# Sparse and linear attention kernel: parts split in PSUM, bf16 bias rows, small PSUM banks re-ordered, one ScalarE instruction for the masked tiles of a unit

## The reference

```python
xn = layernorm(x)
q, k, v = split(xn @ Wqkv.T + bqkv)          # 16 heads of 8
q, k = layernorm(q, q_gamma, q_beta), layernorm(k, k_gamma, k_beta)
aw = softmax(q @ k.T / sqrt(8))
mask = aw >= 12th largest of its row          # top 5% of 256 keys
o_s = (aw * mask / (sum(aw * mask) + 1e-8)) @ v
qf, kf = softmax(q, -1), softmax(k, -1)       # over the 8 channels
o_l = qf @ (kf.T @ v) / (qf . sum(kf) + 1e-6)
o = a * o_s + (1 - a) * o_l                   # a = sigmoid(alpha) per head
y = x + (o @ Wproj.T + bproj) + (xn @ W[idx] + b[idx])
```

## Time and profile before

| | |
|---|---|
| Runs | 1337.95 us median of 3 (1335.01 to 1338.44) |
| Profiled execution, its own time | 1329.16 us |
| Its span, from the first to the last instruction | 1327.4 us |
| Mean granted TensorE clock | 0.926 of full speed |
| Busy share of the span: PE, DVE, ACT, POOL | 79%, 91%, 86%, 82% |
| Bytes moved, mean rate | 83.42 MB, 63 GB/s |

### The profile page before, as it was taken

How to read it: one execution, slowest core, us unless ns; L and a number is a source line. 1 busy time by engine, 2 the same in 40 slices (tenths; PEclk the granted TensorE clock), 3 DMA queues, 4 the chain that set the end, 5 groups by cost and what they waited for, 6 DMA issues and landing times.

```text
span 1327.4 us, 39880 instructions
## 1 busy us (share of the span) xinstructions
PE 1051.5 (79%) x9156; PEld 718.5 (54%) x9156; DVE 1212.3 (91%) x4660; ACT 1135.2 (86%) x3946; POOL 1092.6 (82%) x1618
## 2 busy tenths in 40 slices
PE   3578887878787888887888887788878888887887
PEld 1345555555555555555555555555555555555555
DVE  5789999999899998999989999899989999999994
ACT  3588998998899897998888989788988889998984
POOL 4588888988789887889878889788888888889973
PEclk9979999998899998998989989889998889899998
DMA  2212221222222122221112222112221122221220
GB/s 57 68 45 73 76 77 43 60 65 65 79 77 70 36 64 65 77 77 52 56 53 75 77 77 60 46 53 77 77 79 34 58 65 77 76 77 37 61 58 13
DMA packets 165196, 83.42 MB, mean 63 GB/s; under 512 B 7747, under 2 KB 164933, under 8 KB 164934
## 3 DMA queue, kind: packets, MB, share of 16 engines
q1 hardware_dynamic: 164934, 80.54, 21.1%
HBM read 42.77 MB, written 37.75 MB: 61 GB/s over the span
## 4 chain that ended last, share of the span: by engine, by line
PE 34%; issue 21%; ACT 17%; POOL 13%; DVE 13%; DVEq 1%; POOLq 1%; ACTq 0%; DMA 0%; SPq 0%
PE turn_ps L814 9%; ACT e L705 9%; POOL below L389 8%; DVE rest L510 6%; PE turn_ps L815 4%; DVE top L503 4%; PE work_ps L892 3%; PE work_ps L891 3%; PE pv_ps L831 3%; DVE next L516 3%; PE score_ps L797 2%; PE pv_ps L843 2%; ACT xn L756 2%; PE work_ps L921 2%; ACT below L718 1%
## 5 line engine op out<-in xcount | busy, mean ns | idle before, releaser
L389 POOL TENSOR_SCALAR below<-e,next 128x256 bf16<-128x256 f32 x768 | 695.8, 921 | 0.0
L705 ACT ACTIVATE e<-score_ps,drop 128x256 f32<-128x256 f32 x1024 | 475.4, 492 | 76.1 <-POOL drop L363 75.6
L814 PE MATMUL turn_ps<-ident,e 128*128 128x128 f32 x2048 | 432.8, 304 | 29.1 <-issue 14.5
L510 DVE MATCH_REPLACE8 rest<-e 128x256 f32<-128x256 f32 x1024 | 413.1, 406 | 0.9 <-issue 0.9
L516 DVE MAX8 next<-rest 128x8 f32<-128x256 f32 x1024 | 410.5, 411 | 3.3 <-issue 1.8
L815 PE MATMUL turn_ps<-minus_huge,below 128*128 128x128 bf16 x2048 | 406.4, 234 | 0.0
L503 DVE MAX8 top<-score_ps 128x8 f32<-128x256 f32 x1024 | 360.2, 413 | 37.3 <-PE score_ps L797 19.8
L814 PEld LDWEIGHTS turn_ps<-ident,e 128*128 128x128 f32 x2048 | 314.4, 154 | 97.9 <-issue 31.5
L666 ACT ACTIVATE kept<-turn_ps 128x512 f32<-128x512 f32 x512 | 292.2, 624 | 67.0 <-PE turn_ps L815 62.6
L815 PEld LDWEIGHTS turn_ps<-minus_huge,below 128*128 128x128 bf16 x2048 | 234.7, 115 | 0.0
L705 ACT ACTIVATION_READ_ACCUMULATOR e<-score_ps,drop 128x1 f32 x1024 | 229.3, 224 | 0.0
(11 more groups left out here) (141 smaller groups left out, 1529.7 us busy)
## 6 DMA issues: line engine op xcount, KB each, us to landing
part_slots<-part SPq DMA_DIRECT2D x128, 192.0 KB, 2.3
q_slots<-part_slots SPq DMA_DIRECT2D x64, 256.0 KB, 3.4
k_slots<-part_slots SPq DMA_DIRECT2D x64, 256.0 KB, 4.2
part_slots<-part SPq DMA_DIRECT2D x64, 128.0 KB, 1.9
x_sb<-in_L_attn_x SPq DMA_DIRECT2D x32, 128.0 KB, 4.0
x_res<-in_L_attn_x SPq DMA_DIRECT2D x32, 128.0 KB, 3.9
out_y<-out_sb SPq DMA_DIRECT2D x32, 128.0 KB, 4.3
w_ops<-in_L_ffn_W SPq DMA_DIRECT2D x1, 512.0 KB
```

The lines of the kernel that those rows point to most:

```text
L389: nc.gpsimd.tensor_scalar(below[:, r, t, :], e[:, r, t, :], next8[:, r, t, TOPK - 9:TOPK - 8], None, ALU.is_lt).then_inc(s["below_pool"], 1)
L510: nc.vector.match_replace(rest[:, t, :], e8[:, (u_ - 1) % 2, t, :], e[:, (u_ - 1) % RING, t, :], REMOVED).then_inc(s["rest_ready"], 1)
L705: nc.scalar.activation(e[:, u_ % RING, t, :], score_ps[:, u_ % 2, t // 2, t % 2, :], ACT.Exp, bias=drop[:, u_ % 2, t, 0:1], accum_out=z[:, ...
L814: mm(dst, e[:, r, t, keys], ident[:], start=True, stop=False, is_transpose=True)
```

## The change

- **Parts in PSUM.** `qkT` and `residue` and POOL's two subtractions are gone. ACT casts the first part from `work_ps`; PE then adds minus that part into the same bank (a bf16 matrix with -1 on its diagonal, 512 columns), and ACT casts the second part from there; once more for the third. The transposes into the bank are one accumulation group.
- **Biases.** The three fp32 rows become rows of three partitions holding three bf16 parts of each bias, multiplied by a 3 by 128 block of ones, one bf16 matmul each. DVE makes the parts in the set-up, seven instructions per row (`in_parts`), two of the three rows in `stage_gate`.
- **One sums step.** Both halves of the tokens are transposed in unit 5 (eight transposes, through a permutation that packs nine columns per head, so that both halves fit one bank), and it stands after the scores in PE's list. DVE's three operations are done once, on both halves.
- **Order of the small banks.** The transposed q features go from unit 4 to unit 0, their product from unit 5 to unit 2 (DVE reads it in unit 3, slots 1 and 3, before PE may transpose q and k). The output goes to `pv_ps`: its transposes stay in unit 1, its products go from unit 2 (after the scores) to unit 3 (before the scores).
- **Evacuation.** `kept` of a unit is one instruction over both banks of `turn_ps`, 1024 columns. PE starts a unit's masked tiles when that instruction has ended, and the instruction starts when all of them are there.

```diff
-                        for hh in range(2):
-                            act.wait_ge(s["turn_ready"], 2 * (g - 4) + hh + 1)
-                            nc.scalar.activation(kept[:, u_ % 4, hh], turn_ps[:, hh], ACT.Relu).then_inc(
-                                s["turn_copied"], 1)
+                        act.wait_ge(s["turn_ready"], g - 3)
+                        nc.scalar.activation(kept[:, u_ % 4], turn_ps[:], ACT.Relu).then_inc(s["turn_copied"], 1)
...
-                        wait(act, s["residue_ready"], 2 * (it + 1))
-                        nc.scalar.copy(qkT[:], work_ps[:].rearrange("p (a n) -> p a n", a=2)).then_inc(
-                            s["qkT_copied"], 1)
...
-                    if u_ == 4 and exists(it):
+                    if u_ == 0 and exists(it):
                         act.wait_ge(s["w_qfT"], it + 1)
+                        wait(act, s["w_lin"], it)
                         nc.scalar.copy(qfT[:], work_ps[:, 0:N]).then_inc(s["qfT_copied"], 1)
                     if u_ in (4, 5) and exists(it + 1):
                         p = u_ - 3
-                        act.wait_ge(s["residue_ready"], 2 * (it + 1) + p)
-                        nc.scalar.copy(part[:, p], residue[:, p - 1]).then_inc(s["part_ready"], 1)
+                        act.wait_ge(s["w_rest"], 2 * (it + 1) + p)
+                        nc.scalar.copy(part[:, p], work_ps[:].rearrange("p (a n) -> p a n", a=2)).then_inc(
+                            s["part_ready"], 1)
```

On DVE (set-up and `extra`):

```diff
+            def in_parts(row, cols):
+                p0, p1 = bias_part[:, 0, cols], bias_part[:, 1, cols]
+                r1, r2, total = bias_rest[:, 0, cols], bias_rest[:, 1, cols], bias_sum[:, cols]
+                own = [ident[0:PARTS, p:p + 1] for p in range(PARTS)]
+                setup(nc.vector.tensor_copy(p0, row))
+                setup(nc.vector.tensor_tensor(r1, row, p0, ALU.subtract))
+                setup(nc.vector.tensor_copy(p1, r1))
+                setup(nc.vector.tensor_tensor(r2, r1, p1, ALU.subtract))
+                setup(nc.vector.tensor_scalar(total, p0, own[0], None, ALU.mult))
+                setup(nc.vector.scalar_tensor_tensor(out=total, in0=p1, scalar=own[1], in1=total, op0=ALU.mult,
+                                                     op1=ALU.add))
+                return nc.vector.scalar_tensor_tensor(out=bias3[:, cols], in0=r2, scalar=own[2], in1=total,
+                                                      op0=ALU.mult, op1=ALU.add)
...
-                    if u_ == 5 and 3 <= k <= 5 and exists(it):
+                    if u_ == 3 and k in (1, 3) and exists(it):
...
-                    if u_ in (5, 7) and 1 <= k <= 4 and exists(it - 1):
+                    if u_ == 5 and 1 <= k <= 4 and exists(it - 1):
```

On PE (`mm` is a matmul, `early` comes before the scores of a unit, `late` after):

```diff
                     pe.wait_ge(s["below_act"], (TILES - POOL_TILES) * (g2 + 1))
+                    wait(pe, s["turn_copied"], g2)
                     for hh in range(2):
-                        wait(pe, s["turn_copied"], 2 * (g2 - 1) + hh + 1)
...
+                def sums():
+                    pe.wait_ge(s["pv_copied"], QUADS * it)
+                    for t in range(NT):
+                        for q in range(QUADS):
+                            at = (t * QUADS + q) * 4 * VA
+                            last = nc.tensor.transpose(pv_ps[:, at:at + P], oT[:, nxt, q, t * P:(t + 1) * P], gather[:])
+                    last.then_inc(s["w_turn"], 1)
+                def remainder(p):
+                    pe.wait_ge(s["part_ready"], PARTS * (it + 1) + p + 1)
+                    mm(work_ps[:], minus_one[:], part[:, p].rearrange("p a n -> p (a n)"), start=False,
+                       stop=True, skip_group_check=True).then_inc(s["w_rest"], 1)
...
+                    if u_ == 0 and exists(it):
+                        pe.wait_ge(s["dexp_ready"], 2 * it + 1)
+                        if exists(it + 1):
+                            pe.wait_ge(s["raw_ready"], it + 2)
...
+                    if u_ == 3 and exists(it - 2):
+                        pe.wait_ge(s["osT_copied"], it - 1)
+                        pe.wait_ge(s["pv_copied"], QUADS * it - 1 if exists(it - 1) else QUADS * B)
...
+                            mm(dst, ones3[:], bias3[:, 3 * C:4 * C], start=False, stop=False)
...
+                    if u_ == 5 and exists(it + 1):
+                        remainder(1)
                     if u_ == 6 and exists(it + 1):
...
-                        wait(pe, s["part_ready"], PARTS * (it + 1) + 1)
-                        wait(pe, s["lin_ready"], it + 1)
+                        pe.wait_ge(s["part_ready"], PARTS * (it + 2))
...
-                    if u_ in (5, 7) and exists(it - 1):
-                        sums(u_)
                     early(u_)
                     if exists(it if u_ < UNITS - 1 else it + 1):
                         scores(u_)
+                    if u_ == 5 and exists(it - 1):
+                        sums()
                     late(u_)
```

More of the change, by code:

```diff
@@ L185, in build @@
         oT = sb("oT", [P, 2, QUADS, N])
-        den = sb("den", [P, 2, NT, H])
+        den = sb("den", [P, 2, NT * H])
         o_sparse = sb("o_sparse", [P, NT, C])
@@ L862, in early @@
+                        last.then_inc(s["w_qfT"], 1)
+                    if u_ == 1 and exists(it - 2):
+                        pe.wait_ge(s["osp_ready"], it - 1)
+                        pe.wait_ge(s["lin_ready"], it - 1)
+                        pe.wait_ge(s["pv_copied"], QUADS * it - 2 if exists(it - 1) else QUADS * B)
+                        for t in range(NT):
+                            dst = pv_ps[:, t * P:(t + 1) * P]
                             mm(dst, o_sparse[:, t, :], ident[:], start=True, stop=False, is_transpose=True)
@@ L880, in early @@
                             mm(dst, xnT[:, (xr + 1) % XRING, t * P:(t + 1) * P], w_v[:], start=True, stop=False)
-                            last = mm(dst, ones_row[:], b_row[:, 2 * C:3 * C], start=False, stop=True)
+                            last = mm(dst, ones3[:], bias3[:, 2 * C:3 * C], start=False, stop=True)
                         last.then_inc(s["w_v_ready"], 1)
@@ L891, in early @@
                             mm(dst, xnT[:, (xr + 2) % XRING, t * P:(t + 1) * P], w_qk[:], start=True, stop=False)
-                            last = mm(dst, ones_row[:], b_row[:, 0:2 * C], start=False, stop=True)
+                            last = mm(dst, ones3[:], bias3[:, 0:2 * C], start=False, stop=True)
                         last.then_inc(s["w_qk_ready"], 1)
@@ L929, in late @@
                             for t in range(NT):
-                                last = nc.tensor.transpose(
-                                    work_ps[:, side * N + t * P:side * N + (t + 1) * P],
-                                    qkn[:, (2 * t + side) * C:(2 * t + side + 1) * C], ident[:])
+                                first = side == 0 and t == 0
+                                last = mm(work_ps[:, side * N + t * P:side * N + (t + 1) * P],
+                                          qkn[:, (2 * t + side) * C:(2 * t + side + 1) * C], ident[:],
+                                          start=first, stop=side == 1 and t == NT - 1, is_transpose=True)
                         last.then_inc(s["w_qkT"], 1)
-                    if u_ == 4 and exists(it):
-                        pe.wait_ge(s["kv_ready"], it + 1)
-                        pe.wait_ge(s["dexp_ready"], 2 * it + 1)
-                        if exists(it + 1):
-                            pe.wait_ge(s["part_ready"], PARTS * (it + 1) + 1)
-                        else:
-                            pe.wait_ge(s["y_ready"], it - 1)
-                        for t in range(NT):
-                            last = nc.tensor.transpose(work_ps[:, t * P:(t + 1) * P], q_exp[:, par, t, :], ident[:])
-                        last.then_inc(s["w_qfT"], 1)
+                    if u_ == 4 and exists(it + 1):
+                        remainder(0)
                     if u_ == 6 and exists(it + 2):
```

170 lines of the change are left out of this document (79 added, 91 removed).

## The result

The changed kernel takes 1291.53 us (median of 4 runs, 1290.22 to 1293.94) beside 1336.48 (1329.57 to 1338.44): a ratio of 0.9675, 95% interval 0.9636 to 0.9714. That is 43 us faster by the ratio, 45 by the two medians. The profiled execution took 1291.26 us, 37.9 less than that of before. The direction was forecast; of the size, the forecast 20 us are less than half. The time lies just inside the low end of the range that the prediction gave for 8 in 10, 1290 to 1352.

A forecast was written before the change was run, and what follows sets the result against it. DVE was taken to set the pace, with 2.5 us idle per batch. (-8 + 8 - 8 - 5) x 1.6 = -21, start +3, end -2 gave -20: 1318 us against the median, 8 in 10 within 1290 to 1352.

The forecast's parts named there:

- the three normalising operations: DVE's normalising work, done 20 times at double width instead of 40: -8 us per 20 batches (-6.5 to -9).
- wait before `den`: DVE's wait for `sums`, now behind remainder and scores in unit 5: +8 us per 20 batches (-6 to +34).
- waits of `rest` for `e8`: ACT late at `rest` because masked tiles stood behind output products: -8 us per 20 batches (0 to -8).
- the fourth term: DVE's `top` waiting for PE's scores, shortened by bf16 biases and moved transposes: -5 us per 20 batches (0 to -5).
- the evacuation: ACT's single 1024-column `kept`: taken at 1.1 us, gaining ACT 0 to 0.1 per unit.
- The start: Set-up before the first scores, with bias parts made ahead of `d_max`: +3 us over the run (0 to +8).
- The end: After the last batch, second `sums` round and last output's two bias rows go: -2 us (0 to -3).
- POOL: POOL loses two subtractions of 1.163 us per batch; counted as nothing, only adding to its 6.0 idle.
- The wait before `den` did not vanish with POOL's load: Rival 1: lighter POOL brings `drop` and `oT` sooner and the `den` wait vanishes: 1277 us, chance 0.13.
- The queue wait of 2.6: Rival 3: `sums` queues behind the remainder on PE, 2.6 us every batch, other waits stay: 1381 us, chance 0.13.
- The lock of both banks: Rival 4: `kept` over two banks shuts PE out, 0.48 us at each of 64 waits: 1349 us, chance 0.10.
- half way case of 1297: Half of rival 1, the `den` wait vanishing with a lighter POOL: 1297 us; rival 1 as a whole had chance 0.13.

The follow-up runs named there:

- a_fp32_bias: The changed kernel with the one-partition fp32 bias rows of before: 1337.39 us, ratio 0.9988 to the kernel before.
- b_bf16_bias: The kernel before with only the three bias rows made three bf16 parts, order as before: 1299.57 us, ratio 0.9735.
- b_out_unit3: The kernel before with only the output products moved from unit 2 to unit 3, ahead of its scores, in their old bank: 1330.14 us, ratio 0.9965.
- a_sums_first: The changed kernel with the eight sums transposes put ahead of unit 5's second remainder and scores: 1268.97 us, ratio 0.951 to the kernel before.
- a_old_split: The changed kernel with the parts made by ACT's copy and POOL's two subtractions again: 1304.15 us, ratio 0.9779 to the kernel before.
- a_two_halves: The changed kernel with `kept` as two 512-column instructions, each waiting for its own bank: 1295.45 us, ratio 0.9709 to the kernel before.

## Why the prediction was right and wrong

The forecast's own sum against what was measured, per 20 batches of the stretch of the earlier trace rows, beside what the trace of the change and that of a_fp32_bias give, each scaled to 20 batches (20.75 and 20.09 in the stretch):

| us per 20 batches | forecast | change | change with fp32 biases |
|---|---|---|---|
| the three normalising operations | -8 | -8.0 | -8.3 |
| wait before `den` | +8 | -0.2 | +9.1 |
| waits of `rest` for `e8` | -8 | -8.8 | -8.1 |
| waits of `top` for PE | -5 | -3.2 | +7.5 |
| other waits ("issue" of `top`, `rest`, `next`) | 0 | -4.6 | -1.5 |
| rest of DVE's busy time | 0 | -2.8 | -1.3 |
| sum | -13 | -27.6 | -2.6 |

**The step that failed** is the fourth term, as the prediction put it: "PE's lateness at `top` ... -5 (0 to -5)". It took the fp32 bias rows' worth to be the 5.1 us of idle time that one row of the trace blames on PE's scores, and capped it there, 8 us over the run. The edit saves over one microsecond of PE per batch by the prediction's own figures. Taken out of the change, the same edit costs 46 us of time. What was missed is that PE's lateness sits under other rows too: the two last columns differ by nothing but the bias rows, and the difference of 25 lies in the wait before `den` (9), in that of `top` for PE (11) and in four smaller ones. It was also missed that the lighter chain meets the lower clock less often: about 15 of the 46 us are there at full clock. In its own row the term was not short (-3.2 for -5). Row by row, the 14.6 us that the sum lacks are 8.2 in `den`, 4.6 in the "issue" rows, 2.8 in DVE's busy time and 0.8 in `rest`, less 1.8 in `top`; the third column has `den` near its forecast, so the largest of these is the bias edit under another name.

**The `den` wait, +8**, was sized well and still wrong. In the change with fp32 biases it is 27.7 us in 20 batches, 1.38 each, where I had taken 1.3. With bf16 biases it is 0.92. The prediction listed the chain's links correctly, but did not let ACT and `oT` come earlier with lighter bias rows; with them `oT` comes 0.50 after the first `top` of unit 5 (446.42 and 445.92), where in a batch of a_fp32_bias it comes 0.90 after (465.07 and 464.17). The two terms were treated as independent and are not. The range had a slip besides: it was said to be 1300 to 1332 from the bounds of this term, but -6 and +34 in the prediction's own sum give 1296 and 1360.

**Right by luck in part:** the waits for `e8`, -8.8 for -8. The prediction put them down to the output products ahead of the masked tiles, and read that from 448.04 and 449.32. Those rows lie in the unit 3 with the granted clock at 0.64; in the unit 3 of the next batch the same products stand ahead of the tiles (483.74 to 486.39, full clock) without such a wait. b_bf16_bias leaves the order alone and has 1.7 us of the wait left, b_out_unit3 changes only the order and has 2.5: either is enough.

**Right:** the work of DVE's three normalising operations, to a tenth; the evacuation (1055 ns for "near 1.1"); the eight transposes (1.09 for 1.2); the remainder, 0.39 for an estimated 0.3. The start was 2.4 us later at the first `top`, as forecast within a microsecond, but was regained by the first output, which came 2.0 earlier (133.73 for 135.73); before, a `top` at 79.84 had waited 3.35 behind fp32 products at the lower clock (1.15 us each from 75.59 on). The end gave 3.2 (last output gap 7.8 for 11.0) for a forecast 2. POOL was costed at nothing, and its load is worth 13 us in single batches.

**The rivals.** The wait before `den` did not vanish with POOL's load. It went when `sums` moved (a_sums_first, 0.3 us in the stretch) and when the remainder ahead of it was taken out (a_old_split, 2.0). The queue wait of 2.6 did not come, the wait stayed between 0.6 and 1.9 in the stretch. The lock of both banks has no measurable cost (a_two_halves). The result lies near the half way case of 1297, though not by its mechanism.

**Still open:** why a busy PE chain meets the lower clock in one batch and not in the next (in the changed kernel PE is busy for 4.00 of the 4 us from 466 to 470, at 1.00); how much of the time saved is the clock's; which of the PSUM split, the order and the evacuation gives the 18 us; and the 2.8 us of DVE's busy time, which I put down to instructions that no longer overlap across a wait. b_bf16_bias speaks for it (same DVE work per batch but for the set-up, 37.17 busy per batch for 37.40), but nothing measured it by itself. The 12 us of the "issue" rows (four stretches of up to 3.5 us) were not tried.

## What to carry to other kernels

Price an edit by the chain that it shortens and by what that chain releases, and not by the one idle row that names the engine at its end; here a row of 5.1 us in 20 batches stood for an edit worth 35 us alone and 46 in the end. A tiny bias product in fp32 can cost an in-order engine as much as a full one. When a step is merged and moved, try the merge at the old place too: here the merge gained 20 us alone, and the new place gave back 22. A part that seems to add nothing may be covered by such a loss: with `sums` at its old place the rest of the change was worth 18 us. And look at where the stretches of lower clock lie; the mean clock of a run did not show what they cost here.

## What the runs showed of the hardware

- The fp32 product with weights of one partition takes as long as one of 128 partitions (430 ns per record for 444, in the stretch of the earlier trace rows); three partitions of bf16 take 278 in the same stretch of the changed kernel, in one record instead of two. The Trainium skill (FP8 and Floating Point Precision, TensorE Precision Notes) gives true fp32 four passes through the array; here the two bias products hold PE for 0.62 and 0.21 us at full clock, a ratio of three. These are times of whole products and do not count the passes.
- One ScalarE instruction over 1024 columns and two banks takes 1.055 us, two overlapping ones of 512 take 1.11 as a pair.
- A wait can cost its engine more than its idle time: with the wait of 0.92 us before `den` gone, unit 5 was 1.11 us shorter.
- At the 1.2 GHz level a fp32 product with its two records holds PE for 1.15 us instead of 0.62 (a_fp32_bias, 477.95 to 479.10), and the masked tiles of a unit take 2.70 us instead of 1.47 (kernel before).
